# First routing of a macaron layer: a slot table built on TensorE and gathers from the input, in place of rows scattered to DRAM

## The reference

```python
x = layernorm(input).reshape(T, D)
probs = softmax(x @ w_switch + b_switch)
pmax, routes = probs.max(-1), probs.argmax(-1)
oh = (routes[:, None] == arange(E)[None, :]).astype(int32)
pos = (cumsum(oh, axis=0) * oh).sum(-1) - 1          # place of the token among those of its expert
keep = pos < capacity
slot = where(keep, routes * capacity + pos, E * capacity)
buf = zeros((E * capacity + 1, D)).at[slot].set(x)
h = relu(einsum('ecd,edh->ech', buf_e, w1) + b1)     # 256 -> 1024
y = einsum('ech,ehd->ecd', h, w2) + b2               # 1024 -> 256
out = where(keep, y_flat[slot], x) * pmax / stop_gradient(pmax)
```

## Time and profile before

| | us |
|---|---|
| median of 3 runs | 2294.75 (2292.65 to 2299.19) |
| the profiled execution | 2278.68 |
| its span | 2276.8 |
| PE busy | 2101.2 (92%) |
| DVE busy | 1745.3 (77%) |
| ACT busy | 1702.5 (75%) |
| POOL busy | 944.1 (41%) |

### The profile page before, as it was taken

The page is one execution under the profiler, slowest core; times in us unless marked ns, Lnnn a source line. Parts: engine busy times, 40 slices in busy tenths (PEclk is TensorE's granted clock), DMA queues, the critical chain, the costliest instruction groups (busy, mean ns, idle before and its releaser), DMA issues.

```text
span 2276.8 us, 35911 instructions
## 1 busy us (share of the span) xinstructions
PE 2101.2 (92%) x12776; PEld 1062.3 (47%) x12776; DVE 1745.3 (77%) x2662; ACT 1702.5 (75%) x3309; POOL 944.1 (41%) x1073
## 2 busy tenths in 40 slices
PE   4579965899999999999999999999999999997997
PEld 2369854343444344434434443443434333335896
DVE  7657645788887988888798788879888898726674
ACT  6856643478888888788888878888887887865663
POOL 4755413263383265158227614832661101204441
PEclk7589986899999999999999999999999999999998
DMA  8733511425434433453333434343333444112431
GB/s 271 262 131 131 191 51 54 94 30 132 71 67 106 88 67 104 81 94 76 95 87 67 96 82 87 74 104 65 79 94 58 84 71 96 50 29 92 142 127 50
DMA packets 144994, 218.02 MB, mean 96 GB/s; under 512 B 32128, under 2 KB 101178, under 8 KB 144560
## 3 DMA queue, kind: packets, MB, share of 16 engines
q1 hardware_dynamic: 135216, 197.99, 35.9%
q0 software_dynamic: 9216, 16.95, 2.1%
q10 hardware_dynamic: 384, 0.79, 0.2%
HBM read 129.66 MB, written 84.79 MB: 94 GB/s over the span
## 4 chain that ended last, share of the span: by engine, by line
PE 79%; DVE 10%; ACT 3%; issue 3%; DMA 3%; POOL 2%; SPq 0%; ACTq 0%; POOLq 0%; DVEq 0%
PE PS L968 20%; PE PS L952 19%; PE PS L935 12%; PE PS L879 7%; DVE NMX L1948 5%; PE PS L721 3%; PE PS L910 3%; PE PS L848 3%; PE PS L850 3%; PE PS L849 3%; PE PS L832 2%; PE PS L834 2%; PE PS L833 2%; PE PS L975 1%; DMA NX<-in_x 1%
## 5 line engine op out<-in xcount | busy, mean ns | idle before, releaser
L1948 DVE TENSOR_REDUCE NMX<-PS 128x1 f32<-128x1024 f32 x1024 | 1221.8, 1219 | 241.8 <-PE PS L935 236.8
L1368 ACT ACTIVATE PB<-PS 128x512 f32<-128x512 f32 x2048 | 1098.1, 604 | 209.9 <-PE PS L952 199.3
L952 PE MATMUL PS<-QF,KF 51*128 51x512 f32 x2048 | 791.5, 462 | 6.0 <-ACT SQ L1323 2.9
L935 PE MATMUL PS<-KF,QF 49*128 49x512 f32 x2048 | 705.0, 442 | 21.7 <-DVE NMX L1948 16.0
L952 PEld LDWEIGHTS PS<-QF,KF 51*128 51x128 f32 x2048 | 324.9, 184 | 553.3 <-ACT PB L1368 315.3
L968 PE MATMUL PS<-PB,V 128*17 128x512 f32 x4096 | 540.5, 599 | 0.2
L935 PEld LDWEIGHTS PS<-KF,QF 49*128 49x128 f32 x2048 | 312.2, 186 | 150.0 <-DVE NMX L1948 93.5
L2173 POOL TENSOR_TENSOR R1R<-R,HI 128x512 fp32r<-128x512 f32 x60 | 76.8, 1281 | 199.0 <-ACT R L1334 198.9
L1712 DVE TENSOR_TENSOR HLR<-HL,HHR 128x512 fp32r<-128x512 f32 x128 | 88.8, 694 | 87.5 <-ACT HHR L1297 87.5
L848 PE MATMUL PS<-W2H,HLR 128*128 128x256 f32 x512 | 142.8, 279 | 0.0
L850 PE MATMUL PS<-W2H,HHR 128*128 128x256 f32 x512 | 141.5, 276 | 0.0
(11 more groups left out here) (268 smaller groups left out, 3050.4 us busy)
## 6 DMA issues: line engine op xcount, KB each, us to landing
W<-in_w SPq DMA_DIRECT2D x32, 1024.0 KB, 8.0
QF<-qs SPq DMA_DIRECT2D x186, 128.0 KB, 4.2
KF<-qs SPq DMA_DIRECT2D x186, 128.0 KB, 6.9
qs<-HI SPq DMA_DIRECT2D x64, 256.0 KB, 2.1
qs<-R1R SPq DMA_DIRECT2D x64, 256.0 KB, 2.5
buf<-ZT SPq DMA_DIRECT2D x16, 520.0 KB, 10.5
PX<-x2d SPq DMA_DIRECT2D x8, 1024.0 KB, 5.5
QX<-x2d SPq DMA_DIRECT2D x8, 1024.0 KB, 5.7
```

What stands on the lines that cost most here:

```text
L935: m = e.matmul(PS[:, 2 * i + half, :], QF[k][at:at + ROWS_S, p * SEQ + ti * 128:p * SEQ + ti * 128 + 128], KF[k][at:at + ROWS_S, p * SEQ + ...
L952: e.matmul(PS[:, bank, :], KF[k][at:at + ROWS_ST, p * SEQ + sbk * 128:p * SEQ + sbk * 128 + 128], QF[k][at:at + ROWS_ST, p * SEQ + th * 51 ...
L1368: e.activation(PB[j % 3][:, h * 512:(h + 1) * 512], PS[:, place["e", tile], :], ACT.Exp).then_inc(e_out, 1)
L1948: e.tensor_reduce(NMX[:, u % 2, at:at + 1], PS[:, 2 * i:2 * i + 2, :], AX.XY, ALU.max, negate=True).then_inc(s_max, 1)
```

## The change

- No DRAM slots in the first routing: the zeroing, the 64 scatters and the loads of slots go. Only one DRAM tensor buf is left, for the second routing.
- Instead a table is built. For each batch DVE finds each token's place in its expert (POSF). POOL splits the place into a quarter s (of 128 places) and a place within it (`spread`), and writes UP: for each token 8 experts x 4 quarters x 4 values, zero but for its own, which holds scale, token number, mean and inverse deviation. DVE writes LOW1, for each token a row of 128 with a one at its place (`low_ones`). PE sums LOW1 transposed times UP over all 64 blocks in bank 5 (`table`). The result holds for every slot the four values; DVE reads out the token numbers as integers (PIX) and the values (PLACED).
- POOL gathers the rows of x from the input by PIX, four transfers of 128 rows per expert: experts 0 and 1 at once, expert 2 after XB of expert 1, expert x+3 after the rows of expert x have left (`fetched`).
- Logits come from transposes of x as loaded, with w_switch centred first (PE and DVE at the start), and DVE multiplies the inverse deviation in. ACT's normalization goes. The coefficients AB and the epsilon are POOL's now.
- Counts of earlier batches come through OHS, a bf16 sum of one-hot rows, with eight more small products of PE.
- A load of x5 to x7 waits for the store of its buffer alone. GQ, B1, WP, WPT, WQKV and the first expert's weights are issued ahead of the stores; the second expert's weights after the table.
- ACT's weight splits and WQH stand at position 168 of the order, the tables TA, TB at 178. DVE's weight splits stand behind PIX and PLACED. WQL on POOL stands behind expert 1's XB and expert 2's gathers.
- The order has 262 positions. The warm-up at the start goes (`AGAIN[6]`, nine matmuls); ahead of expert 0 there are 8 matmuls in place of 14.

The diff, cut to its core:

```diff
-    Way(stats=(156, 156, 159, 159, 161, 161, 168, 168), mean=170, ... back=204, shift=206, exp=208, softmax=209,
-        onehot=212, count=215, counted=216, slots=217, own=222, settle=(223, 225, 227, 229), scatter=(223, ...)),
+    Way(stats=(193, 193, 195, 195, 199, 199, 207, 207), mean=210, inverse=212, shift=222, exp=226, softmax=230,
+        onehot=234, count=238, slots=241, own=250, settle=(258, 259, 260, 261), transposes=(182, 185, 186, 189),
+        turned=(196, 197, 201, 203), logits=213, logits_out=216, back=218, low=247, values=246, spread=242,
+        table=249),
...
# SP
             load_x(1)
+            e.dma_start(IOTA[:, :], cst[:, 768 + NT:896 + NT]).then_inc(ld_cst, 16)
             load_x(2)
-            e.wait_ge(set_z, 1)
-            for z in range(zw):
-                zero(0, z)
             load_x(3)
             load_x(4)
...
+            load_w(0)
             for c in range(NB):
                 store_x(c)
                 if c + 5 < NB:
                     e.wait_ge(st_x[c], 16)
-                    for i in range(8):
-                        e.wait_ge(scat[i], 16 * (c + 1))
                     load_x(c + 5)
...
# SP, experts(0)
+                    e.wait_ge(up_out, 2)
+                    e.wait_ge(st_x[4], 16)
+                    load_w(1)
...
# PE, routed(c)
+                for i in range(8):
+                    m = e.matmul(PS[:, UP_BANK, 0:128], LOW1[:, c % 2, i, :], UP[:, c % 2, i, :],
+                                 start=(c == 0 and i == 0), stop=(c == NB - 1 and i == 7))
+                m.then_inc(up_full, 1)
...
# POOL, spread(c)
+                for s in range(1, CT):
+                    m = e.tensor_scalar(STEP[:, q, :, s], pos, 128.0 * s, -128.0, ALU.is_ge, ALU.mult)
...
+                e.tensor_tensor(UP[:, q, :, :].rearrange("p t (e x) -> p t e x", e=8),
+                                one.unsqueeze(3).to_broadcast([128, 8, NE, 4 * CT]),
+                                UPV[:, q, :, :].unsqueeze(2).to_broadcast([128, 8, NE, 4 * CT]), ALU.mult).then_inc(up_val, 1)
...
# POOL, experts(0)
+                def fetched(x):
+                    for s in range(CT if x >= 2 else 0):
+                        placed(e, x - 2, s)
+                    if x >= 3:
+                        e.wait_ge(yo_done, 4 * (x - 2))
+                    for s in range(CT):
+                        e.indirect_dma_start(
+                            out=BUF[x % 3][:, s, 0:D], out_offset=None, in_=x_in,
+                            in_offset=bass.IndirectOffsetOnAxis(ap=PIX[:, x, s:s + 1], axis=0),
+                            bounds_check=T - 1, oob_is_err=False).then_inc(scat[4 * (x % 2) + s], 16)
...
+                    e.wait_ge(up_out, 1)
+                    e.wait_ge(st_x[3], 16)
+                    e.wait_ge(st_x[4], 16)
+                    fetched(0)
+                    fetched(1)
...
# DVE, after the last position
+            e.wait_ge(up_full, NB)
+            table = PS[:, UP_BANK, 0:128].rearrange("p (e s v) -> p e s v", s=CT, v=4)
+            e.tensor_scalar(PIX[:, :, :], table[:, :, :, TKC - SCC], -1.0 / 128, float(T), ALU.mult, ALU.add).then_inc(up_out, 1)
+            e.tensor_scalar(PLACED[:, :, :, :], table, 1.0 / 128, None, ALU.mult).then_inc(up_out, 1)
+            e.wait_ge(up_out, 2)
+            split_w1(0)
+            split_w2(0)
+            for k in range(NB - 1):
                 e.wait_ge(st_x[k], 16)
-            for i in range(8):
-                e.wait_ge(scat[i], 16 * NB)
             experts(0)
...
# DVE
+        def low_ones(e, c):
+            e.tensor_tensor(LOW1[:, c % 2, :, :], IOTA[:, 0:128].unsqueeze(1).to_broadcast([128, 8, 128]),
+                            POSF[:, c % 2, :].unsqueeze(2).to_broadcast([128, 8, 128]), ALU.is_equal).then_inc(up_low, 1)
```

More of the change, by code:

```diff
@@ L63 @@
 MOVED = 2
-Way = namedtuple("Way", "stats mean inverse bias normal transposes turned logits logits_out back shift exp softmax "
-                        "onehot count counted slots own settle scatter")
+Way = namedtuple("Way", "stats mean inverse shift exp softmax onehot count slots own settle transposes turned logits "
+                        "logits_out back low values spread table counted scatter", defaults=(None,) * 11)
 FIRST = (
[L70 to L101, removed]
-)
@@ L103 @@
-FIRST_END = 242
+    Way(stats=(2, 2, 4, 4, 7, 7, 11, 11), mean=13, inverse=16, shift=27, exp=34, softmax=39, onehot=41,
+        count=46, slots=62, own=42, settle=(47, 50, 53, 57), transposes=(1, 3, 6, 9), turned=(5, 8, 10, 12),
+        logits=14, logits_out=18, back=20, low=85, values=87, spread=73, table=98),
+    Way(stats=(15, 15, 17, 17, 19, 19, 21, 21), mean=24, inverse=29, shift=45, exp=60, softmax=66, onehot=71,
+        count=76, slots=82, own=80, settle=(93, 96, 99, 102), transposes=(22, 23, 26, 30), turned=(25, 28, 31,
+        35), logits=38, logits_out=40, back=43, low=133, values=114, spread=105, table=140),
@@ new lines @@
+    Way(stats=(33, 33, 36, 36, 48, 48, 51, 51), mean=59, inverse=64, shift=78, exp=83, softmax=92, onehot=95,
+        count=103, slots=128, own=125, settle=(136, 141, 143, 146), transposes=(32, 44, 49, 52), turned=(37, 61,
+        63, 67), logits=69, logits_out=72, back=75, low=174, values=157, spread=147, table=177),
+    Way(stats=(54, 54, 56, 56, 58, 58, 74, 74), mean=77, inverse=97, shift=132, exp=134, softmax=138,
+        onehot=142, count=145, slots=164, own=167, settle=(181, 184, 188, 192), transposes=(55, 65, 79, 81),
+        turned=(68, 70, 86, 89), logits=108, logits_out=113, back=116, low=202, values=179, spread=175,
+        table=208),
@@ new lines @@
+    Way(stats=(100, 100, 101, 101, 104, 104, 107, 107), mean=115, inverse=131, shift=144, exp=150, softmax=166,
+        onehot=171, count=173, slots=176, own=187, settle=(227, 229, 233, 235), transposes=(84, 88, 90, 94),
+        turned=(91, 106, 109, 111), logits=129, logits_out=135, back=137, low=214, values=200, spread=191,
+        table=220),
+    Way(stats=(110, 110, 112, 112, 118, 118, 120, 120), mean=124, inverse=139, shift=172, exp=180, softmax=183,
+        onehot=190, count=194, slots=205, own=209, settle=(239, 240, 243, 245), transposes=(117, 119, 122, 126),
+        turned=(121, 123, 127, 130), logits=161, logits_out=165, back=169, low=225, values=223, spread=219,
+        table=232),
@@ L329, in build_program @@
         WPT = put("WPT", [128, 2, D])
+        IOTA = put("IOTA", [128, 128])
         nx_at = at[0]
@@ L2264, in gpsimd_program @@
             e.memset(WQKV[:, :, 768 + NE:VC + VW], 0.0).then_inc(set_w, 1)
+            for i in range(2, 4):
+                own.out(e.memset(nx[i][:, :, D:XC], 0.0))
+            for s, fill in ((0, -128.0), (CT, 0.0)):
+                own.out(e.memset(STEP[:, :, :, s], fill))
             side = Side()
```

633 lines of the change are left out of this document (384 added, 249 removed).

## The result

| | before | after |
|---|---|---|
| median of 4 runs each | 2293.7 us (2290.37 to 2299.19) | 2260.1 us (2259.07 to 2261.14) |
| ratio after / before | | 0.9848, 95% interval 0.9833 to 0.9862 |
| profiled execution | 2278.68 | 2259.07 |
| its span | 2276.8 | 2257.3 |
| eighth batch's slots (IDX; POSF) start | 110.67 | 85.40 |

I predicted 2272 (2257 to 2288), and 2255.7 for the profiled execution. The runs gained 33.6 us, the two profiled executions 19.6. That difference is the main thing to explain, since the start of expert 0 came where it was predicted (111).

The account below looks back on a forecast made before the run. TensorE is full from expert 0's first matmul; before it a chain of waits bounds, no engine full. Slots at 90 plus 20.1 plus 1 for the clock give 111, 23 less than 134; median 2294.75 becomes 2272 us, range 2257 to 2288.

Parts of the forecast that it names:

- Expert 0's start: First matmul of expert 0, end of the first routing: from 134.21 to 111 us, a gain of 23 us.
- S at 90: Time when DVE has the eighth batch's slots: 90 us, bounds 80 and 106, with DVE busy 92% of the stretch.
- From S to expert 0: Way from the eighth batch's slots to expert 0's first matmul: 20.1 us plus 1 for the clock, gather landing 3.4.
- Rival C: Gathers behind stores and weights land 6 to 8 us later, or batch 6's store does; gain 16, 2279 us; chance 0.11.
- The experts' pace: Experts behind the first routing: later gathers fit POOL's idle time, so they keep their pace and only move.
- less 23: Last step: the 23 us gain taken from the runs' median of 2294.75, 16 above the profiled execution, giving 2272.
- my own case: Expert 0 starting near 111 us: gain 18 to 28, time 2267 to 2277 us; chance 0.37.
- rival A: First routing runs tighter: slots near 81, expert 0 near 102 us, gain 32, time 2263; chance 0.21.
- B: Fixed queue order and PE at 0.50 to 0.52 clock: slots near 100, expert 0 near 121, gain 13, 2282; chance 0.17.
- D: No change worth the name: slots at 106 plus late gathers, expert 0 near 131, gain 3, 2292 us; chance 0.07.
- E: UP on POOL slow, deciding from 4.6 us per UP; at 6.5, expert 0 at 128 and 2289 us; chance 0.07.
- the 5 us of exclusion: DVE's weight splits shutting out POOL's gather issues for all 5 us: expert 0 near 114 instead of 111.

Follow-up runs that it names:

- e7: Kernel after with 64 activations put back on ACT ahead of the first routing's XTP copies, output unused; median 2271.96 us.
- e5: Kernel after with the first routing's bn_stats over 128 of each row's 256 columns; median 2256.35 us.
- e1: Kernel after with the second expert's weights and B2 issued only once expert 0's four gathers have landed; median 2257.41 us.
- e0: Kernel before, unchanged, profiled and timed again; median 2300.41 us.
- e6: Kernel after with 28 instead of 8 warm-up matmuls between the slot table and expert 0; median 2262.18 us.
- e2: Kernel after with DVE splitting expert 0's weights before it waits for the table; median 2256.71 us.
- e9: Kernel after with UP built for the first four experts alone, 128x512 instead of 128x1024; median 2256.15 us.

## Why the prediction was right, and where it was not

*Expert 0's start, 134.21 to 111*: measured 112.56, 21.65 us in place of 23. Two terms in it were off and cancelled.

*S at 90*: measured 85.6 (POSF's end). DVE's utilization was right (92% against 94%); its work until there was 68 us in place of 71, although LOW1 was under-priced (1.67 against 1.25). But the reason I gave, a stage bound by DVE with ACT "no bound", was wrong: e7 shows ACT's relief worth 11 to 12 us, and in e5 6.8 us less of DVE's work moved the slots by 0.3 to 1.6 us. How much of that is the late load and the slow clock of that execution is open. The eighth load was put near 66 and landed at 62.2; the slots came 23.2 us behind it, where I had counted 13 for an unhindered batch. The other engines were priced too high: until the slots PE was busy 49 us (67 to 80 predicted), POOL 53 (65), ACT 49 (61). Every batch's route passes through ACT, PE, DVE and POOL in a fixed order, and ACT's busy total says nothing of when it must answer.

*From S to expert 0, 21.1 with the clock*: measured 26.9 from POSF's end. Spread and UP 4.9 (4.8), table 3.8 (3.0, bound 3.7), first gather's issue 1.0 us after PIX where I had counted none, fourth issue 5.34 later (5.3), landing 8.54 (3.4), normalizing to expert 0 3.1 (3.35). The failed term is the landing: I priced it by the scatters' own landings with 1.3 us of traffic, and not by the transfers issued in the same microseconds: a store at 99.53, 2 MB of weights at 100.01, B2. Rival C had this mechanism (6 to 8 us late); it came with 5.1, and e1 took 3.8 of it back. The 1 us for the clock did not show ahead of expert 0, whose last step took 3.1.

*The experts' pace*: as predicted, the rest of the span is 2144.7 against 2142.6 and, in e0, 2145.5.

*2272*: the step that failed is the last one, "less 23" from the median. It took the 16 us between the median and the profiled execution as an offset that stays. e0 shows nearly all of it in the first routing of before, in stalls that the kernel after does not have. So the gain is 17 us where before is quick (by e6; after itself was not run there) and 33 to 38 where it is not. The measured 2260.1 lies outside my own case (2267 to 2277): the range holds it only through the far end of rival A, expert 0 near 102, which did not come. That part was luck. The forecast for the profiled execution itself, 2255.7, missed by 3.4.

*Rivals*: A was half right (S between 81 and 90); B's PE clock went the other way, 0.90 on average; D and E did not come: UP takes 1.91 us alone, 2.77 at the most. (E's threshold of 4.6 us is 4.35 by its own sum: 60 + 8 x 4.35 + 16.3 = 111.)

*The port.* The prediction took the stretched issue as "part" of an exclusion. For issues that stands: beside the splits they last 1.72, 1.21 and 1.50 us, at DVE's rest 1.30 for the first (e2) and 1.00 for the others. Two ended and the third began before the splits did (99.79), so the 5 us of exclusion that the prediction held against its order did not come. For whole instructions it was too mild: OHS and LOW1 wait for UP's end, POOL's steps for LOW1's. What the Trainium skill ("SBUF — State Buffer", section "SBUF: two separate sides") says of DVE and GpSimd sharing a port pair that one of them holds at a time agrees with these rows. It does not cover the row at 72.00, where LOW1 started 0.12 us behind POOL's power and lost nothing. e9 puts a price on the meetings here: slots 2.1 to 3.4 us earlier for 0.85 us less of UP per batch, POOL's own shorter list included.

## What to carry to other kernels

When the median lies above the profiled execution, find out where before you subtract from it: profile the kernel twice and compare the start of one landmark in each; a gain can be larger than the profile holds. Price a landing by the transfers issued in the same microseconds, and issue nothing large beside one that the critical chain waits for. Total busy time neither makes an engine the only bound (DVE, 94%) nor clears it (ACT, 67%): put the work back, or take some away, and look, and compare the granted clock and the landings of the two executions before you read the difference.

## What I had not expected of the hardware

- 64-element sums on DVE lasting 1.92 us beside a POOL product, 0.19 alone; bn_stats beside UP keep their pace (2.04 us for six at 66.31, beside UP from 66.41), and so does LOW1 beside POOL's power (1.22 at 72.00).
- Stalls of up to 5.3 us on ACT with no releaser in the profile, in the kernel before alone and on some chips more than others: before takes 2279 on one and 2298 on two, after 2260 in the result and on one of those two. Their cause is open.
- A granted clock that differs between executions of one kernel at a place 300 us behind any edit, worth 6.7 us of 2260.
